# Transposing attention probabilities as 64-row pieces in two passes

## What is computed

```python
# L0, per sequence of 64 tokens
q, k, v = split(where(vm, rms(x) @ v_qkv, rms(x) @ l_qkv))          # 16 heads of 16, rotary on q and k
p = softmax(causal(q @ k.T / 4)); ctx = p @ v
h = x + where(vm, ctx @ v_dense, ctx @ l_dense)
cq = rms(h) @ cq_w; ck, cv = split(ctx_1024 @ ckv_w)                # 16 heads of 8
p = softmax(cq @ ck.T / sqrt(8)); h = h + (p @ cv) @ cdense_w
h = h + where(vm, mlp_v(rms(h)), mlp_l(rms(h)))                     # silu(gate) * up, 688 wide, then down
# L1: attention of h over the context (W_mem), a sigmoid gate, a residual, rmsnorm
```

## Time and profile before

| | us |
|---|---|
| median of 3 runs | 533.59 |
| lowest, highest | 533.56, 535.44 |
| the profiled execution's own time | 532.92 |
| its span, first to last instruction | 531.1 |

### The profile page before, as it was taken

One profiled execution on the slowest core, in us unless ns is written; L12 is line 12 of the kernel. 1 busy time (PEld: TensorE's weight loads), 2 busy tenths in 40 slices (PEclk: granted clock), 3 DMA queues, 4 the chain that ended last, 5 costly groups with the idle time before them and its releaser, 6 DMA issues. The chain is left out here.

```text
span 531.1 us, 10845 instructions
## 1 busy us (share of the span) xinstructions
PE 458.8 (86%) x3974; PEld 362.9 (68%) x3974; DVE 360.8 (68%) x788; ACT 252.7 (48%) x694; POOL 146.8 (28%) x262
## 2 busy tenths in 40 slices
PE   0579687999999999999999999999996894988993
PEld 0457465877877686868778687877875694866772
DVE  4787988675886778587768848775875362266455
ACT  4165643454454456363544635454453340555664
POOL 6163312023112302320330212023111112265453
PEclk9995989799999999999999999999999798899998
DMA  7544510001011001100020110011000031021111
GB/s 210 160 149 122 147 41 31 11 22 60 12 41 41 31 1 41 52 21 12 31 70 3 40 51 22 11 32 42 10 12 33 27 110 40 21 69 61 51 60 40
DMA packets 22691, 27.13 MB, mean 51 GB/s; under 512 B 3280, under 2 KB 19408, under 8 KB 22640
## 3 DMA queue, kind: packets, MB, share of 16 engines
q1 hardware_dynamic: 20992, 22.08, 13.4%
q0 software_dynamic: 1648, 4.36, 2.6%
HBM read 19.74 MB, written 6.68 MB: 50 GB/s over the span
## 5 line engine op out<-in xcount | busy, mean ns | idle before, releaser
L1015 DVE TENSOR_REDUCE mx<-xyz 128x8 f32<-128x512 f32 x64 | 43.7, 683 | 7.5 <-PE xyz L1339 7.5
L684 ACT ACTIVATE vb<-xyz,rstd 64x128 f32<-64x128 f32 x64 | 23.5, 367 | 50.3 <-PE xyz L1317 38.9
L1339 PE MATMUL xyz<-kT,qT 32*64 32x128 f32 (+1 forms) x768 | 44.0, 329 | 3.7 <-ACT qT L721 0.4
L1017 DVE TENSOR_TENSOR E<-xyz,mx 128x512 f32<-128x512 f32 x64 | 44.3, 692 | 2.2
L1364 PE MATMUL xyz<-cst,E 128*128 128x128 f32 x256 | 38.5, 286 | 8.3 <-ACT E L694 4.7
L1190 POOL TENSOR_TENSOR var<-ss,pow_eps 128x1 f32<-128x1 f32 x32 | 6.4, 201 | 135.4 <-ACT att L663 113.6
L1364 PEld LDWEIGHTS xyz<-cst,E 128*128 128x128 f32 x256 | 28.8, 144 | 17.4 <-ACT E L727 8.7
L1494 PE MATMUL b_ps<-w_gu_hi,ms_hi 128*128 (+2 forms) x90 | 38.2, 425 | 0.8 <-ACT ms_hi L751 0.6
L1378 PEld LDWEIGHTS xyz<-vb,kT 128*64 128x64 f32 x1024 | 35.1, 149 | 5.5 <-issue 3.6
L1378 PE MATMUL xyz<-vb,kT 128*64 128x18 f32 (+1 forms) x1024 | 37.7, 228 | 1.2 <-DVE kT L1066 1.2
L763 ACT ACTIVATE th<-b_ps,mrh 128x256 f32<-128x256 f32 (+1 forms) x45 | 20.2, 450 | 34.2 <-PE b_ps L1497 33.8
(11 more groups left out here) (268 smaller groups left out, 1287.0 us busy)
## 6 DMA issues: line engine op xcount, KB each, us to landing
xm<-h_rows SPq DMA_DIRECT2D x17, 128.0 KB, 2.0
h_rows<-xm SPq DMA_DIRECT2D x17, 128.0 KB, 1.7
xT<-in_xT_dram SPq DMA_DIRECT2D x8, 256.0 KB, 3.1
x_sb<-in_x_dram SPq DMA_DIRECT2D x8, 256.0 KB, 2.8
ctxT_a<-in_ctxT_dram SPq DMA_DIRECT2D x8, 128.0 KB, 2.3
over_xs<-in_ctxT_dram SPq DMA_DIRECT2D x4, 256.0 KB, 4.3
out_dram<-late SPq DMA_DIRECT2D x8, 128.0 KB, 1.7
out_dram<-over_qkv SPq DMA_DIRECT2D x8, 128.0 KB, 1.7
```

Of the source, the lines that this page charges most:

```text
L684: act.activation(vb[t][e * SEQ:(e + 1) * SEQ, b, :, e, 0:HD], v[rows, :, e, :], ACT.Copy, scale=rstd[rows, 0, t:t + 1]).then_inc(S["vb_rea ...
L1015: dve.tensor_reduce(mx[:, t, heads], s, AX.X, ALU.max).then_inc(max_ready, 1)
L1017: dve.tensor_tensor(E[t][:, b * 512:(b + 1) * 512].rearrange("p (h k) -> p h k", k=SEQ), s, mx[:, t, heads].unsqueeze(2).to_broadcast([P, ...
L1339: last = pe.matmul(xy[t][q, hp, o:o + w], qT[t][rows, c, q], kT[t][rows, (2 * c + b) * w:(2 * c + b + 1) * w], start=not masked, stop=True ...
```

## The change

The eight 128 x 128 transpositions of a tile become sixteen pieces. A piece takes 64 rows of E (one sequence) and two heads, so 128 columns stay stationary and 64 identity columns move. Pieces alternate between the upper and the lower 64 rows of the array, and neighbours write different banks. In the first pass (`probT_a`) the upper rows write bank X and the lower rows bank Y; in the second (`probT`) the banks are swapped, and it waits for the first pass's end by a new semaphore `pTa_ps`. The first pass waits for both exp halves. ACT's and DVE's copies both wait for the end of the second pass. The cross attention is changed in the same way.

The steps `probT_a` and `cprobT_a` are new in PE's order, and all orders of all stages are written anew; that of W4 is shown. One wait is added for DVE in the first group (`cdense`: all routes made). No step of arithmetic is added or dropped elsewhere.

```diff
-            def turn_probs(n, t, exp_ready, psx, psy):
-
-                for a in range(PAIRS):
-                    if a % 4 == 0:
-                        pe.wait_ge(exp_ready, half(n, t, a // 4))
-                    last = pe.transpose(xy[t][:, a // 4, (a % 4) * P:(a % 4 + 1) * P], E[t][:, a * P:(a + 1) * P], ident)
-                    if a == 3:
-                        last.then_inc(psx, 1)
-                last.then_inc(psy, 1)
+            def turn_probs(t, turn):
+
+                for a in range(PAIRS // 2):
+                    for b in range(2):
+                        rows = slice(b * SEQ, (b + 1) * SEQ)
+                        bank = (b + turn) % 2
+                        pair = bank * PAIRS // 2 + a
+                        last = pe.transpose(xy[t][:, bank, a * P + b * SEQ:a * P + (b + 1) * SEQ], E[t][rows, pair * P:(pair + 1) * P],
+                                            ident[rows, rows])
+                return last
+
+            def probT_a(n, t):
+                pe.wait_ge(S["exp_ready"], half(n, t, 1))
+                turn_probs(t, 0).then_inc(S["pTa_ps"], 1)
 
             def probT(n, t):
-                turn_probs(n, t, S["exp_ready"], S["pT_psx"], S["pT_psy"])
+                pe.wait_ge(S["pTa_ps"], tl(n, t))
...
+            def cprobT_a(n, t):
+                pe.wait_ge(S["cexp"], half(n, t, 1))
+                turn_probs(t, 0).then_inc(S["cpTa_ps"], 1)
+
             def cprobT(n, t):
-                turn_probs(n, t, S["cexp"], S["cpT_psx"], S["cpT_psy"])
+                pe.wait_ge(S["cpTa_ps"], tl(n, t))
+                turn_probs(t, 1).then_inc(S["cpT_ps"], 1)
 
...
-                act.wait_ge(S["pT_psx"], tl(n, t))
+                act.wait_ge(S["pT_ps"], tl(n, t))
...
-                dve.wait_ge(S["pT_psy"], tl(n, t))
+                dve.wait_ge(S["pT_ps"], tl(n, t))
...
             ("W4", dict(
                 sp="""
-                    load_xT:10 m_in:5 m_in:6 load_ca:10 load_x:10 m_out:5 m_out:6""",
+                    load_xT:10 m_in:5 m_in:6 load_ca:10 m_out:5 m_out:6 load_x:10""",
                 act="""
-                    qkT:8 qkT:9 miT:5 m_sq:5 gu0:5 score:8 gu1:5 probT:8 score:9 gu2:5 probT:9 m_sq:6 hT0:5 xsplit:10
-                    hT1:5 miT:6 ctxT:8 gu0:6 ctxT:9 gu1:6 h1T:8 gu2:6 cproj:8 hT0:6 dense:8 dense:9 h1T:9 cproj:9
-                    hT1:6 cscore:8 cprobT:8 cscore:9 cprobT:9 cctxT:8 cctxT:9 xsq:10 rope:10 xsq:11 rope:11""",
+                    qkT:8 miT:5 m_sq:5 qkT:9 gu0:5 score:8 xsplit:10 gu1:5 m_sq:6 probT:8 score:9 gu2:5 hT0:5 probT:9
+                    hT1:5 ctxT:8 miT:6 ctxT:9 h1T:8 dense:8 cproj:8 gu0:6 dense:9 h1T:9 cproj:9 gu1:6 cscore:8 gu2:6
+                    cprobT:8 hT0:6 cscore:9 hT1:6 cprobT:9 cctxT:8 cctxT:9 xsq:10 rope:10 xsq:11 rope:11""",
                 dve="""
-                    qkT:8 qkT:9 miT:5 score:8 gu0:5 score:9 gu1:5 probT:8 gu2:5 hT0:5 probT:9 hT1:5 pv:8 down:5 pv:9
-                    miT:6 ctxT:8 xsplit:10 ctxT:9 dense:8 gu0:6 gu1:6 dense:9 gu2:6 hT0:6 cscore:8 hT1:6 cscore:9
-                    cprobT:8 cprobT:9 cpv:8 cpv:9 cdense:8 down:6 cdense:9 xsq:10 xsq:11 rope:10 rope:11""",
+                    qkT:8 qkT:9 miT:5 score:8 gu0:5 score:9 probT:8 gu1:5 gu2:5 pv:8 hT0:5 probT:9 hT1:5 ctxT:8 pv:9
+                    down:5 miT:6 dense:8 ctxT:9 xsplit:10 dense:9 gu0:6 cscore:8 gu1:6 cscore:9 cprobT:8 hT0:6 gu2:6
+                    cpv:8 cprobT:9 hT1:6 down:6 cpv:9 cdense:8 cdense:9 xsq:10 xsq:11 rope:10 rope:11""",
                 pool="""
-                    m_sq:5 m_sq:6 dense:8 dense:9 xsplit:10 sort:8 xsq:10 xsq:11 rope:10 sort:9 rope:11""",
+                    m_sq:5 m_sq:6 dense:8 xsplit:10 dense:9 sort:8 xsq:10 xsq:11 rope:10 rope:11 sort:9""",
                 pe="""
-                    qkT:8 miT:5 qkT:9 score_a:8 score:8 gu0:5 score_a:9 score:9 gu1:5 probT:8 gu2:5 probT:9 hT0:5 pv:8
-                    hT1:5 down:5 pv:9 miT:6 ctxT:8 gu0:6 dense:8 ctxT:9 gu1:6 dense:9 h1T:8 gu2:6 cproj:8 hT0:6
-                    cscore_a:8 h1T:9 cscore:8 cproj:9 hT1:6 cscore_a:9 cscore:9 cprobT:8 down:6 cprobT:9 cpv:8 cpv:9
-                    cctxT:8 cdense:8 cctxT:9 qkvv:10 cdense:9 qkv:10 qkv:11 qkvv:11""",
+                    qkT:8 miT:5 qkT:9 score_a:8 score:8 gu0:5 score_a:9 score:9 gu1:5 probT_a:8 probT:8 gu2:5 pv:8
+                    hT0:5 probT_a:9 hT1:5 probT:9 ctxT:8 down:5 miT:6 pv:9 dense:8 ctxT:9 gu0:6 h1T:8 dense:9 cproj:8
+                    cscore_a:8 h1T:9 cscore:8 cproj:9 gu1:6 cscore_a:9 cscore:9 gu2:6 cprobT_a:8 cprobT:8 hT0:6 cpv:8
+                    cprobT_a:9 hT1:6 cprobT:9 down:6 cctxT:8 cpv:9 cdense:8 cctxT:9 qkvv:10 cdense:9 qkv:10 qkv:11
+                    qkvv:11""",
...
             ("MID", dict(
                 sp="""
-                    m_in:13 m_in:15 m_in:14 m_out:13 m_in:16 load_cb:0 m_out:14 m_out:15 m_out:16""",
+                    load_cb:0 m_in:13 m_in:15 m_in:14 m_out:13 m_in:16 m_out:14 m_out:15 m_out:16""",
...
```

More of the change, by code:

```diff
@@ L327, in xattn_kernel @@
                 act="""
[L328 to L331, removed]
+                    wsplit:0 xsplit:0 wsplit:1 wsplit:2 wsplit:3 xsq:0 wsplit:4 wsplit:5 wsplit:6 xsq:1 wsplit:7
@@ L335, in xattn_kernel @@
[L335 to L338, removed]
+                    wsplit:0 first_routes:0 xsplit:0 pos:0 route_t:0 table:0 xsq:0 wsplit:1 wsplit:2 wsplit:3 rank:0
@@ L347, in xattn_kernel @@
+                    cprobT_a:1 cprobT:1 fold:0 cpv:1 cctxT:1 cdense:1 qkv:3 qkvv:3""",
             )),
@@ L385, in xattn_kernel @@
+                    cscore_a:4 h1T:5 cscore:4 cproj:5 gu1:2 cscore_a:5 cscore:5 gu2:2 cprobT_a:4 cprobT:4 hT0:2 cpv:4
+                    cprobT_a:5 hT1:2 cprobT:5 down:2 cctxT:4 cpv:5 cdense:4 cctxT:5 qkvv:6 cdense:5 qkv:6 qkv:7 qkvv:7""",
             )),
@@ L404, in xattn_kernel @@
+                    cscore_a:6 h1T:7 cscore:6 cproj:7 gu1:4 cscore_a:7 cscore:7 gu2:4 cprobT_a:6 cprobT:6 hT0:4 cpv:6
+                    cprobT_a:7 hT1:4 cprobT:7 down:4 cctxT:6 cpv:7 cdense:6 cctxT:7 qkvv:8 cdense:7 qkv:8 qkv:9 qkvv:9""",
             )),
@@ L444, in xattn_kernel @@
+                    cprobT_a:10 cprobT:10 hT0:8 cpv:10 cprobT_a:11 hT1:8 cprobT:11 down:8 cctxT:10 cpv:11 cdense:10
+                    cctxT:11 qkvv:12 cdense:11 qkv:12 qkv:13 qkvv:13""",
             )),
@@ L463, in xattn_kernel @@
-                    gu2:10 cproj:12 hT0:10 cscore_a:12 h1T:13 cscore:12 cproj:13 hT1:10 cscore_a:13 cscore:13
-                    cprobT:12 down:10 cprobT:13 cpv:12 cpv:13 cctxT:12 cdense:12 cctxT:13 qkvv:14 cdense:13 qkv:14
-                    qkv:15 qkvv:15""",
+                    qkT:12 miT:9 qkT:13 score_a:12 score:12 gu0:9 score_a:13 score:13 gu1:9 probT_a:12 probT:12 gu2:9
+                    pv:12 hT0:9 probT_a:13 hT1:9 probT:13 ctxT:12 down:9 miT:10 pv:13 dense:12 ctxT:13 gu0:10 h1T:12
@@ L466, in xattn_kernel @@
+                    dense:13 cproj:12 cscore_a:12 h1T:13 cscore:12 cproj:13 gu1:10 cscore_a:13 cscore:13 gu2:10
+                    cprobT_a:12 cprobT:12 hT0:10 cpv:12 cprobT_a:13 hT1:10 cprobT:13 down:10 cctxT:12 cpv:13 cdense:12
+                    cctxT:13 qkvv:14 cdense:13 qkv:14 qkv:15 qkvv:15""",
             )),
```

228 lines of the change are left out of this document (115 added, 113 removed).

## The result

The changed kernel takes 549.87 us (median of 4 runs, 548.84 to 554.62), the kernel before 533.58 beside it: ratio 1.032, interval 1.025 to 1.039. It is 16.3 us slower where +6 was forecast, outside my range. The profiled execution took 550.26 us, with a span of 548.4 and a mean granted clock of 0.939 (before: 532.92, 531.1 and 0.960).

What follows compares the result with a forecast made beforehand. PE's own order was taken to bound W2 to W6. Seven windows at +0.9 us (pieces +0.55, old waits -1.35, new +2.4, lowered by a walk) and -0.3 elsewhere took 532.9 to 538.9 us; own range 534 to 545, with rivals 527 to 548.

Steps and rivals of the forecast that it cites:

- rival 3: Pieces don't run at double pace (single file, or loads twice as long): pass 0.43 instead of 0.23, 549 us; chance 0.12.
- The two large waits: New PE waits in W4: `cpv:8` for DVE's copy, +1.1 us, and `cscore_a:8` for ACT's copy behind `cproj:8`, +0.4.
- the three small ones: New PE waits in W4, all on DVE: `pv:8` +0.2 us, `h1T:9` +0.4, `cctxT:9` +0.3.
- My period of 48.6 a window: W2 to W6: the period, 47.7 us now, should be near 48.6; the prediction is wrong if it falls.
- the walk's 0.6: Walking through the window with each engine's order gave +0.6 us, against +1.6 by summing; +0.9 was taken.
- The pieces' own part, 0.55: On PE, per window: slower passes of pieces +0.36 us and two more shape changes at `cpv:8` and `cpv:9` +0.19.
- `load_x` costed at 0: SP's load of x behind `m_out`, landing 2.8 us after issue: hidden by PE's work; without that cover up to 1.0 a window.
- Four issues, waiting for nothing late: MID: `load_cb` moved ahead of `m_in:13`, costed at nothing, with 0 to 2 us once.
- the middle of W0, MID and L1 together: Only orders move in these stages: taken as -0.3 us, bounds -3 and +3.
- 1 (the order wins): DVE runs earlier, so new waits don't come and old ones are gone: -0.8 us a window, 527.3 us; chance 0.26.
- the old waits: Three PE waits in W4, forecast to go: `cprobT:8` 0.53 us, `cdense:8` 0.59, `cscore_a:9` 0.22; sum -1.35.
- 2 falls: Rival 2, a draw: waits cancel and the slot costs 0 to 0.3 us a window, 533 to 535 us; chance 0.18.

Runs made afterwards that it cites:

- e3: The changed kernel with `load_x` put back ahead of `m_out` in SP's order, in W1 to W7: 546.7 us.
- e6: The changed kernel with whole transpositions instead of pieces, its new orders kept, and `load_x` back ahead of `m_out`: 538.2 us.
- e1: The changed kernel with whole 128-row transpositions instead of pieces, all its new orders kept: 547.5 us.
- e8: The changed kernel with five unused 512-column matmuls on PE ahead of the wait of `cpv`, first tile of each pair: 546.5 us.
- e15: The changed kernel with `load_x` back ahead of `m_out`, the wait of `cpv` filled with unused matmuls, and MID and L1 in their old orders: 537.6 us.
- e13: The kernel before with the changed kernel's order in MID alone: 538.1 us.
- e5: The kernel before, except that a transposition of 8 whole tiles waits for both exps at its start: 540.8 us.
- e12: The kernel before with its old orders and pieces, each pass doing the four of one row half, then the four of the other: 552.7 us.
- e4: The changed kernel with the kernel before's orders in MID and L1: 549.5 us.
- e11: The changed kernel with `load_x` back ahead of `m_out`, and the wait of `cpv` and the pauses of MID and L1 filled with unused matmuls: 540.3 us.
- e10: The kernel before with the changed kernel's W0 orders, and unused matmuls filling PE's two longest DMA waits, ahead of `miT:13` and `h3T:0`: 532.2 us.

## Why the prediction was wrong

**The pieces were right.** A slot was forecast at 1.01 us, a pass at 0.23 to its last start and 0.45 in length; the rows show 0.24 and 0.46, and 0.92 from a slot's first start to the next step's, which with the 0.09 of the way in is 1.01. The 64-row loads don't set a slower pace. The Trainium skill ("TensorE: Matmul & The Clock Gate", LDWEIGHTS) gives columns / 1.2 ns a load, 107 ns for 128 columns. By it the last start would be, as an estimate, 3 x 0.107 = 0.32 behind the first (the 0.43 and the 10 us of my rival 3 fit single file; by the page they would be 0.32 and, also an estimate, 28 x 2 x 0.09 = 5 us); at 0.24 the measurement decides against the page here. Rival 3, at 549, had the right number by a wrong mechanism: that the total came out there is no evidence for it.

**The two large waits were right, the three small ones didn't come.** `cpv:8` was forecast at +1.1 and waits 0.98; `cscore_a:8` at +0.4 waits 0.4 (L1344 for ACT, in each window). `pv:8` (+0.2), `h1T:9` (+0.4) and `cctxT:9` (+0.3) show no wait in W2 to W7. My period of 48.6 a window was for orders and pieces alone, and these came out at 48.22 (e3): 0.5 instead of 0.9 over the old 47.7, nearer to the walk's 0.6 than to what I took. The pieces' own part, 0.55, is 0.16 (e3 against e6), because the wait at `cpv:8` ends when DVE ends, whatever PE did before it: it is 1.0 us with pieces and 1.2 without.

**The first step that failed: `load_x` costed at 0.** I had its bound (1.0 a window), the right chain and the right issue: 263.3 on the old timetable is 36.2 us into the window, and in windows without a fall of the clock it was 36.1. The term that failed is the landing. I took the earlier trace rows's median of 2.8 us as sure, and the cover by `qkv` and `qkvv` was just enough for it, as e1's W4 and W5 show (no cost); but x lands after 2.8 to 3.9 us, and each tenth beyond 2.8 was paid: 2.7 to 3.0 us in W2 to W7, 0.5 a window in the mean.

**The second: the granted clock was taken as given.** The earlier trace rows shows 1.00, and I read it as a state of these windows. It hung, as e8 shows, on PE being at work. I forecast a gap of 1.1 us just there, beside work of little weight, and asked what waits for PE but not what the gap does to PE. The price is 4.6 us with `load_x` late, the largest single term; with `load_x` back it is 1.4 (e3 less e15), since e3 has one fall instead of three.

**The third: MID and L1.** "Four issues, waiting for nothing late" is true of `load_cb` and beside the point: it isn't the issue that costs but 1 MB on the DMA engines when the scatter starts (5.24 us instead of 2.44 in e13). I had 0 to 2, it is 2.4. L1's order added 2.1. I had put the middle of W0, MID and L1 together at -0.3, for no better reason than that orders seemed neutral, and bounded it at +3 (of which my range took in only +1); MID and L1 alone came to 4.5.

**W0.** Nothing of a gain is shown.

By rivals: 1 (the order wins) falls, as the old waits did go but the orders still cost 2.0 with whole transpositions (e6); 2 falls; the forecast's mechanism, the waits that pieces and orders make on PE, is there and makes up 3 of the 16.3 us. The range was too narrow because it was built from PE's waits only.

## What to carry to other kernels

A new wait of about 1 us on a busy TensorE can have two prices, the wait and the clock after it: where the engine was gapless at clock 1.00, give the slow stretch a place in the range, and try to fill the wait with matmuls that nobody needs. When a load moves behind another step of its queue and its cover is just enough for the median landing, cost the landings above the median too, and ask what else is then on the DMA engines. And a change that forces a pass to wait for both halves of an input should be costed with that wait in the old order first (e5: 0.9 us a window, half of what the pieces cost under the old orders).

## What the runs showed of the hardware

- Pieces start two at a time even when those of one row half stand together in the program (e12): 1.02 us for 16 against 0.99, the two starts of a pair 0.013 us apart against 0.003.
- The granted clock falls to 0.5 in and after pauses of 4.1 us (MID, before) and 6.7 us (after). It also falls after waits of 0.9 to 1.0 us in some windows with pieces, in none of e1 and e6 with whole transpositions behind waits of 1.2 us; and once after waits of 0.64 and 0.32 us with no piece near (e4). Which windows it hits differs from kernel to kernel with the same windows (after: W2, W4, W7; e3: W4 alone; both with the same wait); why is open.
- Filled with 512-column bf16 matmuls, waits of 1 us (e8, e11, e15) and the pauses of MID (e10) no longer lower it; where the fill left 2.7 us of MID's pause open (e11), it fell to 0.67.
- 1 MB of loads makes a scatter of 128 KB beside it land after 5.2 us instead of 2.4 (e13).
- A load of 256 KB issued at the same place of the order lands after 2.8 to 3.9 us from window to window (e1).
- In one order of its steps W1 takes 43.6 to 47.4 us, at a mean granted clock from 1.00 down to 0.89.
